# Two scans in a gated recurrence: the denominator formed in the scan's own buffer, and the key-value product moved behind the reciprocal

## The chip, the cores and the metric

One core of one Trainium2 chip runs the kernel. The time is the device time of one execution in microseconds (us), the median over runs. The engines are called PE or TensorE (matrix products; PEld is its weight loads), DVE or VectorE, ACT or ScalarE, POOL or GpSimd, and SP (it issues the DMAs).

## What is computed

The input is 8 sequences of 2048 tokens with 512 channels, in float32. A layer of gated exponential recurrence comes first, then a gated feed-forward layer, each with its residual and layer norm. The part that matters here:

```python
rkv = inputs @ W_rkv + b_rkv
r, k, v = split(rkv, 3)
r = sigmoid(r); k = exp(k); kv = k * v
# over the tokens, with one decay lam per channel
u1 = scan(lam, kv); u2 = scan(lam, k)
x = (u1 + gamma * kv) / (u2 + gamma * k + 1e-06) * r
y = layernorm(inputs + x @ W_o + b_o)
```

The feed-forward layer mixes each token of y with the one before it, takes a receptance sigmoid(xr @ W_r), keys relu(xk @ W_k) squared, and values from them through W_v.

## The kernel before

The 16384 tokens are cut into 32 blocks of 512. A block's channels stand on the 128 partitions in four chunks c = 0 to 3, the tokens in the free dimension. Each matrix product is made of float32r parts: an operand is split into a high part (a copy by ACT) and a low part (value less high part, by POOL or DVE), and a product is high x high, high x low and low x high, so a projection of one chunk is 4 x 3 = 12 matmuls of 512 columns.

**Banks.** The projections of a block are numbered n = 3c + which, with which = 0 for K, 1 for V and 2 for R, and go to PSUM bank n % 4 (`bankA`). In `project` (L1070 and on) the projection n waits until the one four places earlier has been read: K by the exponential on ACT (`key_exp`), V by the product on DVE (`kv_made`), R by the exponential of the gate on ACT (`gate_exp`).

**DVE, per chunk.** `denominator(s, c)`: the scan of the keys into `u2` (L864), the product kv = (V + bias) x key, read from PSUM (L869), a copy of u2's last column into `carry` (L872), the denominator gamma x key + u2, written over the key (L875), its product with 1 + exp(-r), which is called the gate and written in place (L879), and the reciprocal of that (L882). `numerator(s, c)`: the scan of kv into `att_f` (L890), its copy (L893) and u1 + gamma x kv (L895). The gate comes from ACT (`exp_gate`, L609 and L612), which needs the R projection of the same chunk.

**ACT and POOL.** POOL multiplies numerator and reciprocal (`att`, L413) and makes low parts (`att_low` L417, `x_low` L408, `mixed_keys_low` L440, `mixed_gate_low` L445 for xr_lo, `weight_A_low` L397, `weight_low` L403). ACT makes high parts (`att_high` L616) and the squares of the keys (`key_square`, L700 to L704).

**Order.** Each engine's order is written out by hand, in three functions per engine: `first_block`, `step` (block s beside the rest of block s - 1 and s - 2, 30 times) and `finale`. TensorE's `step` is

```python
project(s, 0, 0) ... project(s, 1, 0); attention_out(s1, 0); attention_out(s1, 1)
project(s, 1, 1); project(s, 1, 2); project(s, 2, 0); transposes(s1)
project(s, 2, 1); project(s, 2, 2); project(s, 3, 0); keys(s1)
project(s, 3, 1); receptance(s1, 0); project(s, 3, 2)
values(s1, 0); receptance(s1, 1); values(s1, 1)
```

In `first_block` the twelve projections follow each other with nothing between. In `finale` the five from (2, 1) to (3, 2) follow the transposes with nothing between; then come `keys(s1)`, the first half of `receptance(s1)` and `attention_out(s)`. Every instruction waits on its engine in that order, so a waiting one holds all behind it.

Of the kernel before, what the change touches and what calls it, by code (L numbers as in the profile page):

```python
# [24 lines left out]
ALU = mybir.AluOpType  # L25
# [4 lines left out]
NC = H // P  # L30
TB = 512
# [45 lines left out]
def wait(eng, sem, value):  # L77
    if value is not None:
        eng.wait_ge(sem, value)
# [23 lines left out]
def program(nc, xT, x, w_rkv, w_o, w_r, w_k, w_v, b_rkv, b_o, nu_log, gamma_log, mu_r, mu_k, out, seq):  # L103
# [9 lines left out]
    with ExitStack() as ctx:  # L113
# [446 lines left out]
        def _(act):  # L560
# [34 lines left out]
            def exp_key(s, c):  # L595
                act.wait_ge(k_ready, s.count(NC, c + 1))
                if s.first() and c == 0:
                    act.wait_ge(s_small, 80)

                wait(act, scale_made, s.count(NC, c - 1))  # L600
                act.activation(key[:, c % 2], bankA[(3 * c) % NBANK][:], ACT.Exp, bias=b_sb[:, 0, c:c + 1])\  # L601
                    .then_inc(key_exp, 1)

# [228 lines left out]
        def _(dve):  # L832
# [25 lines left out]
            def denominator(s, c):  # L858
                lam_c = lam[:, c:c + 1].to_broadcast([P, TB])
                dve.wait_ge(key_exp, s.count(NC, c + 1))  # L860

                wait(dve, u2_saved, s.count(NC, c))
                wait(dve, den_made, s.count(NC, c))
                dve.tensor_tensor_scan(u2[:], lam_c, key[:, c % 2], state(s, 1, c), ALU.mult, ALU.add)\  # L864
                    .then_inc(u2_scanned, 1)
                dve.wait_ge(v_ready, s.count(NC, c + 1))

                wait(dve, num_made, s.count(NC, c))
                dve.scalar_tensor_tensor(out=kv[:], in0=bankA[(3 * c + 1) % NBANK][:], scalar=b_sb[:, 1, c:c + 1],  # L869
                                         in1=key[:, c % 2], op0=ALU.add, op1=ALU.mult).then_inc(kv_made, 1)  # L870
                dve.wait_ge(u2_scanned, s.count(NC, c + 1))
                dve.tensor_copy(carry[:, 1, c:c + 1], u2[:, TB - 1:TB]).then_inc(u2_saved, 1)  # L872

                dve.wait_ge(kv_made, s.count(NC, c + 1))
                dve.scalar_tensor_tensor(out=key[:, c % 2], in0=key[:, c % 2], scalar=gamma[:, c:c + 1], in1=u2[:],  # L875
                                         op0=ALU.mult, op1=ALU.add).then_inc(den_made, 1)
                dve.wait_ge(den_made, s.count(NC, c + 1))
                dve.wait_ge(gate_plus1, s.count(NC, c + 1))
                dve.scalar_tensor_tensor(out=gate[:, c % 2], in0=key[:, c % 2], scalar=EPS_DEN, in1=gate[:, c % 2],  # L879
                                         op0=ALU.add, op1=ALU.mult).then_inc(scale_made, 1)  # L880
                dve.wait_ge(scale_made, s.count(NC, c + 1))
                dve.reciprocal(gate[:, c % 2], gate[:, c % 2]).then_inc(rec_made, 1)  # L882

            def numerator(s, c):
                lam_c = lam[:, c:c + 1].to_broadcast([P, TB])
# [83 lines left out]
            def first_block(s):  # L969
                weight_A_low(0, 0)  # L970
                x_low(s, 0)
                x_low(s, 1)
                x_low(s, 2)
                x_low(s, 3)
                weight_A_low(0, 1)
                constants()
                weight_A_low(0, 2)
                gamma_minus1()
                denominator(s, 0)
                numerator(s, 0)  # L980
                denominator(s, 1)
                numerator(s, 1)
                denominator(s, 2)
                numerator(s, 2)
                denominator(s, 3)
                numerator(s, 3)

            def step(s):
                s1, s2 = (s.back(1), s.back(2))
                if s2.exists():  # L990
                    gated_values(s2, 1)
                begin_sum(s1, 0)
                begin_sum(s1, 1)
                denominator(s, 0)
                if s2.exists():
                    statistics(s2, 1, 1, result_rows, y2_made)
                statistics(s1, 0, 0, sum_rows, ready['WO'])
                statistics(s1, 0, 1, sum_rows, ready['WO'])
                numerator(s, 0)
                denominator(s, 1)  # L1000
                mix_keys(s1)
                mix_gate(s1, 0)
                numerator(s, 1)
                denominator(s, 2)
                key_low(s1, 0)
                numerator(s, 2)
                key_low(s1, 1)
                key_low(s1, 2)
                key_low(s1, 3)
                mix_gate(s1, 1)  # L1010
                denominator(s, 3)
                gated_values(s1, 0)
                statistics(s1, 1, 0, result_rows, y2_made)
                x_low(s.back(-1), 0)
                x_low(s.back(-1), 1)
                x_low(s.back(-1), 2)
                x_low(s.back(-1), 3)
                numerator(s, 3)

            def finale(s):  # L1020
                s1, s2 = (s.back(1), s.back(2))
                begin_sum(s1, 0)
                gated_values(s2, 1)
                begin_sum(s1, 1)
                denominator(s, 0)
                statistics(s1, 0, 0, sum_rows, ready['WO'])
                statistics(s2, 1, 1, result_rows, y2_made)
                statistics(s1, 0, 1, sum_rows, ready['WO'])
                numerator(s, 0)
                denominator(s, 1)  # L1030
                numerator(s, 1)
                mix_gate(s1, 0)
                mix_keys(s1)
                denominator(s, 2)
                numerator(s, 2)
                denominator(s, 3)
                numerator(s, 3)
                begin_sum(s, 0)
                begin_sum(s, 1)
                statistics(s, 0, 0, sum_rows, ready['WO'])  # L1040
                key_low(s1, 0)
                key_low(s1, 1)
                key_low(s1, 2)
                key_low(s1, 3)
                mix_gate(s1, 1)
                statistics(s, 0, 1, sum_rows, ready['WO'])
                gated_values(s1, 0)
                mix_keys(s)
                mix_gate(s, 0)
                gated_values(s1, 1)  # L1050
                statistics(s1, 1, 0, result_rows, y2_made)
                key_low(s, 0)
                key_low(s, 1)
                mix_gate(s, 1)
                key_low(s, 2)
                key_low(s, 3)
                statistics(s1, 1, 1, result_rows, y2_made)
                gated_values(s, 0)
                gated_values(s, 1)
                statistics(s, 1, 0, result_rows, y2_made)  # L1060
                statistics(s, 1, 1, result_rows, y2_made)
                last_rows(s)
# [213 lines left out]
```

## Time and profile before

| | us |
|---|---|
| median of 3 runs | 2534.48 |
| lowest and highest | 2532.93, 2536.94 |
| the profiled execution | 2535.74 |
| its span, first to last instruction | 2533.9 |
| PE busy, DVE busy | 2510.5, 2013.6 |
| ACT busy, POOL busy | 1267.5, 1245.6 |

A matmul's row shows its start and its modelled length; matmuls are pipelined and overlap, so what counts is the distance from one start to the next. The note in brackets behind a row is the time the engine sat idle before it and what ended that.

### The profile page before, as it was taken

Reading aid. Unit: us, or ns where it says so; the run is one execution under the profiler, and the core shown is the slowest. Engines: PE = TensorE matmul, PEld = TensorE weight load, DVE = VectorE, ACT = ScalarE, POOL = GpSimd, SP = SyncE. Lnnn points to the kernel's source line nnn. Section 1 sums busy time; section 2 is a strip of 40 time slices with the busy share of each in tenths; the row PEclk is TensorE's granted clock in tenths of the full one; section 3 lists DMA queues with packets and bytes.
Section 4 is the critical chain, followed back from the end, with each engine's and each line's share of the span. In section 5 each row is a group of like instructions: output and inputs, shape, how many; then the busy total and the mean of one; then the engine's idle time right before and its main releaser. Section 6 shows DMA issues by size and latency. Waiting matters only on the chain.

```text
span 2533.9 us, 32904 instructions
## 1 busy us (share of the span) xinstructions
PE 2510.5 (99%) x11268; PEld 2076.7 (82%) x11268; DVE 2013.6 (79%) x2693; ACT 1267.5 (50%) x2157; POOL 1245.6 (49%) x1128
## 2 busy tenths in 40 slices
PE   7999999999999999999999999999999999999998
PEld 6888888888888888888888888888888888888877
DVE  7877888778787787887788777878777888787885
ACT  4545455444554444554545544455444555454545
POOL 6654454445454544535445444444444453545545
PEclk8999999999999999999999999999999999999999
DMA  4001110111100111111111011111111111110100
GB/s 170 26 34 51 45 39 34 34 51 50 34 34 34 51 51 34 46 38 35 51 39 45 34 35 50 50 34 34 35 50 50 34 43 34 43 51 34 51 25 34
DMA packets 57784, 110.63 MB, mean 44 GB/s; under 512 B 7040, under 2 KB 7040, under 8 KB 57088
## 3 DMA queue, kind: packets, MB, share of 16 engines
q1 hardware_dynamic: 57600, 108.31, 12.6%
q8 instruction: 100, 1.64, 0.3%
q14 instruction: 84, 0.69, 0.1%
HBM read 74.73 MB, written 33.55 MB: 43 GB/s over the span
## 4 chain that ended last, share of the span: by engine, by line
PE 98%; ACT 1%; POOL 0%; DVE 0%; DMA 0%; issue 0%; POOLq 0%; SPq 0%; DVEq 0%; ACTq 0%
PE bankA L1086 14%; PE bankA L1088 14%; PE bankA L1087 14%; PE bankB L1102 14%; PE bankB L1104 13%; PE bankB L1103 13%; PE bankB L1147 4%; PE bankB L1148 4%; PE bankB L1146 4%; PE bankB L1124 2%; PE bankA L1102 0%; PE bankA L1104 0%; PE bankA L1103 0%; POOL x_lo L408 0%; DMA wrkv_f<-in_w_rkv 0%; PE bankA L1148 0%
## 5 line engine op out<-in xcount | busy, mean ns | idle before, releaser
L1086 PE MATMUL bankA<-x_hi,wrkv_hi 128*128 128x512 f32 x1488 | 583.9, 392 | 4.7 <-POOL x_lo L408 4.7
L1088 PE MATMUL bankA<-x_hi,wrkv_lo 128*128 128x512 f32 x1488 | 580.5, 390 | 0.0
L1087 PE MATMUL bankA<-x_lo,wrkv_hi 128*128 128x512 f32 x1488 | 580.4, 390 | 0.0
L882 DVE RECIPROCAL gate<-gate 128x512 f32<-128x512 f32 x128 | 429.2, 3353 | 4.4
L413 POOL TENSOR_TENSOR att_f<-att_f,gate 128x512 f32<-128x512 f32 x128 | 209.4, 1636 | 280.1 <-DVE att_f L895 280.1
L1086 PEld LDWEIGHTS bankA<-x_hi,wrkv_hi 128*128 128x128 f32 x1488 | 280.3, 188 | 63.8 <-POOL x_lo L408 5.8
L1088 PEld LDWEIGHTS bankA<-x_hi,wrkv_lo 128*128 128x128 f32 x1488 | 280.1, 188 | 58.7
L1087 PEld LDWEIGHTS bankA<-x_lo,wrkv_hi 128*128 128x128 f32 x1488 | 280.4, 188 | 57.2
L424 POOL TENSOR_TENSOR ve<-mv,eps_ln 128x2 f32<-128x2 f32 x128 | 66.4, 519 | 462.6 <-DVE mv L907 459.6
L440 POOL TENSOR_TENSOR xk_lo<-xk_f,xk_hi 128x512 fp32r<-128x512 f32 x124 | 169.4, 1397 | 244.9 <-ACT xk_hi L667 244.9
L445 POOL TENSOR_TENSOR xr_lo<-xr_f,xr_hi 128x1024 fp32r<-128x1024 f32 x63 | 176.4, 2800 | 202.7 <-ACT xr_hi L672 202.7
L659 ACT ACTIVATE z<-z,shift,rstd 128x512 f32<-128x512 f32 x124 | 94.5, 809 | 297.6 <-POOL shift L433 297.6
L935 DVE SCALAR_TENSOR_TENSOR xr_f<-zT,vecs,xr_f 128x256 f32<-128x256 f32 x252 | 143.3, 628 | 123.7 <-ACT xr_f L644 123.7
L601 ACT ACTIVATE key<-bankA,b_sb 128x512 f32<-128x512 f32 x128 | 87.8, 686 | 283.9 <-PE bankA L1088 283.9
L879 DVE SCALAR_TENSOR_TENSOR gate<-key,gate 128x512 f32<-128x512 f32 x128 | 119.7, 935 | 125.4 <-ACT gate L612 123.2
L417 POOL TENSOR_TENSOR att_lo<-att_f,att_hi 128x512 fp32r<-128x512 f32 x128 | 186.8, 1460 | 32.8 <-ACT att_hi L616 32.8
L1102 PE MATMUL bankB<-wr_hi,xr_hi 128*128 128x512 f32 x504 | 199.5, 396 | 1.1 <-POOL xr_lo L445 1.1
L1103 PE MATMUL bankB<-wr_lo,xr_hi 128*128 128x512 f32 x504 | 196.4, 390 | 0.0
L1104 PE MATMUL bankB<-wr_hi,xr_lo 128*128 128x512 f32 x504 | 196.3, 389 | 0.0
L1102 PE MATMUL bankB<-wo_hi,att_hi 128*128 128x512 f32 x496 | 192.9, 389 | 0.0
L1103 PE MATMUL bankB<-wo_lo,att_hi 128*128 128x512 f32 x496 | 192.9, 389 | 0.0
L1104 PE MATMUL bankB<-wo_hi,att_lo 128*128 128x512 f32 x496 | 192.9, 389 | 0.0
(150 smaller groups left out, 5588.5 us busy)
## 6 DMA issues: line engine op xcount, KB each, us to landing
y<-in_x SPq DMA_DIRECT2D x128, 256.0 KB, 2.7
x_f<-in_xT SPq DMA_DIRECT2D x124, 256.0 KB, 4.0
out<-z SPq DMA_DIRECT2D x124, 256.0 KB, 2.1
wrkv_f<-in_w_rkv SPq DMA_DIRECT2D x3, 768.0 KB, 7.7
xk_f<-in_xT SPq DMA_DIRECT2D x4, 256.0 KB, 4.5
wo_f<-in_w_o SPq DMA_DIRECT2D x1, 1024.0 KB, 11.2
wk_f<-in_w_k SPq DMA_DIRECT2D x1, 1024.0 KB, 13.1
wr_f<-in_w_r SPq DMA_DIRECT2D x1, 1024.0 KB, 15.2
```

The lines of the kernel that those rows point to most:

```text
L413: pool.tensor_tensor(att_f[:, c], att_f[:, c], gate[:, c % 2], ALU.mult).then_inc(att_made, 1)
L417: pool.tensor_tensor(att_lo[:, c], att_f[:, c], att_hi[:, c], ALU.subtract).then_inc(att_lo_made, 1)
L440: pool.tensor_tensor(lo[:, c], value[:, c], hi[:, c], ALU.subtract).then_inc(xk_lo_made, 1)
L445: pool.tensor_tensor(lo[:], value[:], hi[:], ALU.subtract).then_inc(xr_lo_made, 1)
L882: dve.reciprocal(gate[:, c % 2], gate[:, c % 2]).then_inc(rec_made, 1)
L935: dve.scalar_tensor_tensor(out=value[:, c], in0=zT[:, c, HALF * half + 1:HALF * half + HALF + 1], scalar=vecs[:, 2, c:c + 1], in1=value[:, ...
L1086: pe.matmul(bank[:], w_hi, hi[:, h], start=(h == 0), stop=False)
L1087: pe.matmul(bank[:], w_hi, lo[:, h], start=False, stop=False)
L1088: last = pe.matmul(bank[:], w_lo, hi[:, h], start=False, stop=(h == NC - 1))
L1102: pe.matmul(bank[:], hi, w_hi[:, c], start=(c == 0 and not begun), stop=False, skip_group_check=begun)
L1103: pe.matmul(bank[:], hi, w_lo[:, c], start=False, stop=False, skip_group_check=begun)
L1104: last = pe.matmul(bank[:], lo, w_hi[:, c], start=False, stop=(c == NC - 1), skip_group_check=begun)
```

## The change

The four DVE instructions of the denominator now follow the key scan directly, and the denominator is written into `u2`, the scan's own buffer, so that the key stays whole. The product kv moves into a function of its own, `product`, which every order calls straight behind `denominator`; it stands there behind the reciprocal. The scan of a chunk waits for the gate's product of the chunk before (`scale_made`), which is now u2's last reader. On ACT the exponential of a key, which writes the key's buffer, waits for `den_made` and `kv_made` of two chunks earlier in place of `scale_made`.

```diff
@@ exp_key
-                wait(act, scale_made, s.count(NC, c - 1))
+                wait(act, den_made, s.count(NC, c - 1))
+                wait(act, kv_made, s.count(NC, c - 1))
@@ denominator
-                wait(dve, u2_saved, s.count(NC, c))
-                wait(dve, den_made, s.count(NC, c))
+                wait(dve, scale_made, s.count(NC, c))
                 dve.tensor_tensor_scan(u2[:], lam_c, key[:, c % 2], state(s, 1, c), ALU.mult, ALU.add)\
                     .then_inc(u2_scanned, 1)
+                dve.wait_ge(u2_scanned, s.count(NC, c + 1))
+                dve.tensor_copy(carry[:, 1, c:c + 1], u2[:, TB - 1:TB]).then_inc(u2_saved, 1)
+                dve.wait_ge(u2_saved, s.count(NC, c + 1))
+                dve.scalar_tensor_tensor(out=u2[:], in0=key[:, c % 2], scalar=gamma[:, c:c + 1], in1=u2[:],
+                                         op0=ALU.mult, op1=ALU.add).then_inc(den_made, 1)
+                dve.wait_ge(den_made, s.count(NC, c + 1))
+                dve.wait_ge(gate_plus1, s.count(NC, c + 1))
+                dve.scalar_tensor_tensor(out=gate[:, c % 2], in0=u2[:], scalar=EPS_DEN, in1=gate[:, c % 2],
+                                         op0=ALU.add, op1=ALU.mult).then_inc(scale_made, 1)
+                dve.wait_ge(scale_made, s.count(NC, c + 1))
+                dve.reciprocal(gate[:, c % 2], gate[:, c % 2]).then_inc(rec_made, 1)
+
+            def product(s, c):
                 dve.wait_ge(v_ready, s.count(NC, c + 1))
+                dve.wait_ge(key_exp, s.count(NC, c + 1))
 
                 wait(dve, num_made, s.count(NC, c))
                 dve.scalar_tensor_tensor(out=kv[:], in0=bankA[(3 * c + 1) % NBANK][:], scalar=b_sb[:, 1, c:c + 1],
                                          in1=key[:, c % 2], op0=ALU.add, op1=ALU.mult).then_inc(kv_made, 1)
-                dve.wait_ge(u2_scanned, s.count(NC, c + 1))
-                dve.tensor_copy(carry[:, 1, c:c + 1], u2[:, TB - 1:TB]).then_inc(u2_saved, 1)
-
-                dve.wait_ge(kv_made, s.count(NC, c + 1))
-                dve.scalar_tensor_tensor(out=key[:, c % 2], in0=key[:, c % 2], scalar=gamma[:, c:c + 1], in1=u2[:],
-                                         op0=ALU.mult, op1=ALU.add).then_inc(den_made, 1)
...
@@ the orders, at each of the twelve calls of denominator
                 denominator(s, 0)
+                product(s, 0)
```

How DVE's order moves, first in the first block, chunk 0 and the start of chunk 1. Before:

```order
L864 SCALAR_TENSOR_TENSOR u<-lam,key 128x512
L869 SCALAR_TENSOR_TENSOR kv<-bankA,b_sb,key 128x512
L872 COPY carry<-u 128x1
L875 SCALAR_TENSOR_TENSOR key<-key,gamma,u 128x512
L879 SCALAR_TENSOR_TENSOR gate<-key,gate 128x512
L882 RECIPROCAL gate<-gate 128x512
L890 SCALAR_TENSOR_TENSOR att_f<-lam,kv 128x512
L893 COPY carry<-att_f 128x1
L895 SCALAR_TENSOR_TENSOR att_f<-kv,gamma,att_f 128x512
L864 SCALAR_TENSOR_TENSOR u<-lam,key 128x512
L869 SCALAR_TENSOR_TENSOR kv<-bankA,b_sb,key 128x512
```

And with the change (lines are those of the changed kernel):

```order
L864 SCALAR_TENSOR_TENSOR u<-lam,key 128x512
L867 COPY carry<-u 128x1
L869 SCALAR_TENSOR_TENSOR u<-key,gamma,u 128x512
L873 SCALAR_TENSOR_TENSOR gate<-u,gate 128x512
L876 RECIPROCAL gate<-gate 128x512
L883 SCALAR_TENSOR_TENSOR kv<-bankA,b_sb,key 128x512
L892 SCALAR_TENSOR_TENSOR att_f<-lam,kv 128x512
L895 COPY carry<-att_f 128x1
L897 SCALAR_TENSOR_TENSOR att_f<-kv,gamma,att_f 128x512
L864 SCALAR_TENSOR_TENSOR u<-lam,key 128x512
L867 COPY carry<-u 128x1
```

The row of kv went from behind the first scan to behind the reciprocal, ahead of the numerator's scan.

In the last block, on DVE, from the reciprocal of chunk 1 to that of chunk 2 (xr_f and xk_f are the gate and key mixing of the block before). Before:

```order
L882 RECIPROCAL gate<-gate 128x512
L890 SCALAR_TENSOR_TENSOR att_f<-lam,carry,kv 128x512
L893 COPY carry<-att_f 128x1
L895 SCALAR_TENSOR_TENSOR att_f<-kv,gamma,att_f 128x512
L935 SCALAR_TENSOR_TENSOR xr_f<-zT,vecs,xr_f 128x256 x4
L927 SCALAR_TENSOR_TENSOR xk_f<-zT,vecs,xk_f 128x512 x4
L864 SCALAR_TENSOR_TENSOR u<-lam,carry,key 128x512
L869 SCALAR_TENSOR_TENSOR kv<-bankA,b_sb,key 128x512
L872 COPY carry<-u 128x1
L875 SCALAR_TENSOR_TENSOR key<-key,gamma,u 128x512
L879 SCALAR_TENSOR_TENSOR gate<-key,gate 128x512
L882 RECIPROCAL gate<-gate 128x512
```

And with the change:

```order
L876 RECIPROCAL gate<-gate 128x512
L883 SCALAR_TENSOR_TENSOR kv<-bankA,b_sb,key 128x512
L892 SCALAR_TENSOR_TENSOR att_f<-lam,carry,kv 128x512
L895 COPY carry<-att_f 128x1
L897 SCALAR_TENSOR_TENSOR att_f<-kv,gamma,att_f 128x512
L937 SCALAR_TENSOR_TENSOR xr_f<-zT,vecs,xr_f 128x256 x4
L929 SCALAR_TENSOR_TENSOR xk_f<-zT,vecs,xk_f 128x512 x4
L864 SCALAR_TENSOR_TENSOR u<-lam,carry,key 128x512
L867 COPY carry<-u 128x1
L869 SCALAR_TENSOR_TENSOR u<-key,gamma,u 128x512
L873 SCALAR_TENSOR_TENSOR gate<-u,gate 128x512
L876 RECIPROCAL gate<-gate 128x512
```

The kv of chunk 1 came into this stretch, ahead of the numerator of chunk 1, and the kv of chunk 2 moved out of it, behind its last row. On TensorE nothing moves.

## Rows read from the trace of the kernel before

**Rows 1.** The page: engine totals, and the chain that ended last, by engine.

```profile
PE 2510.5 (99%) x11268; PEld 2076.7 (82%) x11268; DVE 2013.6 (79%) x2693; ACT 1267.5 (50%) x2157; POOL 1245.6 (49%) x1128
...
PE 98%; ACT 1%; POOL 0%; DVE 0%; DMA 0%; issue 0%; POOLq 0%; SPq 0%; DVEq 0%; ACTq 0%
```

**Rows 2.** TensorE's waits: released by, us in total, times, longest.

```profile
PE bankA L1086 <- POOL x_lo L408: 4.7, 2, 4.1
```

**Rows 3.** TensorE's timeline, first block: start, length, instruction, [idle before <-releaser].

```profile
23.37 0.39 PE L1086 MATMUL bankA<-xk_hi,wrkv_hi 128*128 128x512 f32 x1
...
23.60 0.39 PE L1087 MATMUL bankA<-xk_lo,wrkv_hi 128*128 128x512 f32 x1
...
31.53 0.39 PE L1086 MATMUL bankA<-xk_hi,wrkv_hi 128*128 128x512 f32 x1
...
43.89 0.77 PE L1086 MATMUL bankA<-xk_hi,wrkv_hi 128*128 128x512 f32 x1 [4.04 <-POOL wrkv_lo L397]
```

**Rows 4.** DVE, first block: both reciprocals; kv's line over the run, ns min/median/max.

```profile
L869 DVE SCALAR_TENSOR_TENSOR kv<-bankA,b_sb,key x128: 718/726/731, 16.0 to 2452.8; 128x512 f32<-128x512 f32 x128
...
20.67 3.35 DVE L882 RECIPROCAL gate<-gate 128x512 f32<-128x512 f32 x1
...
30.34 3.35 DVE L882 RECIPROCAL gate<-gate 128x512 f32<-128x512 f32 x1
```

**Rows 5.** ACT's timeline, first block: the exponential of chunk 3's key.

```profile
37.17 0.69 ACT L601 ACTIVATE key<-bankA,b_sb 128x512 f32<-128x512 f32 x1 [1.36 <-PE bankA L1088]
```

**Rows 6.** Two stretches: PE, PEld, DVE, ACT, POOL busy (instructions), granted clock, DMA, GB/s.

```profile
43.90:49.30 5.40, 5.40 (x13) 4.24 (x14) 5.25 (x7) 0.00 (x0) 4.14 (x2) 0.50 0.00 0
...
2457.60:2466.00 8.40, 6.50 (x28) 5.03 (x28) 7.34 (x8) 7.22 (x14) 4.07 (x3) 1.00 0.23 62
```

**Rows 7.** A middle block: DVE's reciprocal of chunk 1, TensorE's R of chunk 2.

```profile
2352.88 3.35 DVE L882 RECIPROCAL gate<-gate 128x512 f32<-128x512 f32 x1
...
2357.45 0.39 PE L1086 MATMUL bankA<-x_hi,wrkv_hi 128*128 128x512 f32 x1
```

**Rows 8.** Middle block: DVE, POOL, TensorE at the receptance; then last block, DVE and POOL.

```profile
2384.33 1.28 DVE L864 TENSOR_TENSOR_SCAN u<-lam,carry,key 128x512 f32<-128x512 f32 x1
...
2387.08 0.69 DVE L879 SCALAR_TENSOR_TENSOR gate<-key,gate 128x512 f32<-128x512 f32 x1
...
2387.23 2.80 POOL L445 TENSOR_TENSOR xr_lo<-xr_f,xr_hi 128x1024 fp32r<-128x1024 f32 x1 [6.68 <-ACT xr_hi L672]
...
2390.09 0.49 PE L1102 MATMUL bankB<-wr_hi,xr_hi 128*128 128x512 f32 x1
...
2390.42 0.39 PE L1103 MATMUL bankB<-wr_lo,xr_hi 128*128 128x512 f32 x1
...
2455.27 3.35 DVE L882 RECIPROCAL gate<-gate 128x512 f32<-128x512 f32 x1
...
2456.34 2.37 POOL L445 TENSOR_TENSOR xr_lo<-xr_f,xr_hi 128x1024 fp32r<-128x1024 f32 x1
```

**Rows 9.** Last block: DVE, TensorE and ACT.

```profile
2441.34 1.27 DVE L864 TENSOR_TENSOR_SCAN u<-lam,carry,key 128x512 f32<-128x512 f32 x1
...
2445.99 3.35 DVE L882 RECIPROCAL gate<-gate 128x512 f32<-128x512 f32 x1
...
2458.54 1.26 DVE L890 TENSOR_TENSOR_SCAN att_f<-lam,carry,kv 128x512 f32<-128x512 f32 x1
...
2443.98 0.39 PE L1086 MATMUL bankA<-x_hi,wrkv_hi 128*128 128x512 f32 x1
...
2458.86 0.47 PE L1102 MATMUL bankB<-wr_hi,xr_hi 128*128 128x512 f32 x1 [1.12 <-POOL xr_lo L445]
...
2465.34 0.47 PE L1102 MATMUL bankA<-wo_hi,att_hi 128*128 128x512 f32 x1 [0.78 <-POOL att_lo L417]
...
2457.78 0.60 ACT L700 ACTIVATE xk_f<-bankB 128x512 f32<-128x512 f32 x1 [3.15 <-PE bankB L1148]
...
2463.23 0.62 ACT L616 ACTIVATE att_hi<-att_f 128x512 fp32r<-128x512 f32 x1
```

More of the change, by code:

```diff
@@ L870, in denominator @@
                                          in1=key[:, c % 2], op0=ALU.add, op1=ALU.mult).then_inc(kv_made, 1)
-                dve.wait_ge(u2_scanned, s.count(NC, c + 1))
-                dve.tensor_copy(carry[:, 1, c:c + 1], u2[:, TB - 1:TB]).then_inc(u2_saved, 1)
-                dve.wait_ge(kv_made, s.count(NC, c + 1))
-                dve.scalar_tensor_tensor(out=key[:, c % 2], in0=key[:, c % 2], scalar=gamma[:, c:c + 1], in1=u2[:],
-                                         op0=ALU.mult, op1=ALU.add).then_inc(den_made, 1)
[L877 to L882, printed above, removed]
             def numerator(s, c):
@@ L979, in first_block @@
                 denominator(s, 0)
+                product(s, 0)
                 numerator(s, 0)
                 denominator(s, 1)
+                product(s, 1)
                 numerator(s, 1)
                 denominator(s, 2)
+                product(s, 2)
                 numerator(s, 2)
                 denominator(s, 3)
+                product(s, 3)
                 numerator(s, 3)
@@ L994, in step @@
                 denominator(s, 0)
+                product(s, 0)
                 if s2.exists():
@@ L1000, in step @@
                 denominator(s, 1)
+                product(s, 1)
                 mix_keys(s1)
@@ L1004, in step @@
                 denominator(s, 2)
+                product(s, 2)
                 key_low(s1, 0)
@@ L1011, in step @@
                 denominator(s, 3)
+                product(s, 3)
                 gated_values(s1, 0)
@@ L1025, in finale @@
                 denominator(s, 0)
+                product(s, 0)
                 statistics(s1, 0, 0, sum_rows, ready['WO'])
@@ L1030, in finale @@
                 denominator(s, 1)
+                product(s, 1)
                 numerator(s, 1)
@@ L1034, in finale @@
                 denominator(s, 2)
+                product(s, 2)
                 numerator(s, 2)
                 denominator(s, 3)
+                product(s, 3)
                 numerator(s, 3)
```

## The prediction

> **What bounds the kernel now.** I read the engine totals first, then the chain that ended last, and then what TensorE waited for. TensorE is busy 99% of the span and 98% of the chain is its own [rows 1]. Its longest waits stand in the first block: 4.7 us in two for x_lo [rows 2] and 4.04 us for a low part of the projection weights [rows 3]; in the last block one of 1.12 and one of 0.78 us follow [rows 9]. Elsewhere its matmuls start every 0.227 us (23.37 to 23.60 [rows 3]), and DVE, ACT and POOL run beside them. So the change, which adds and removes no instruction, can only cost time where TensorE comes to wait longer, and only give time where it waits now. 0.2% of the time, 5.1 us, is about what a measurement here tells from no change.
>
> **What moves.** The product kv (L869 before) stood second in each chunk, behind the scan; now it stands behind the reciprocal. kv_made is not only read by the numerator: it also frees the bank of V for the projection four places later. K, V and R of chunks 0 to 3 are twelve projections of 12 matmuls (2.72 us each at 0.227), so kv of chunk 0 gates R of chunk 1, kv of chunk 1 gates R of chunk 2, kv of chunk 2 gates R of chunk 3, and kv of chunk 3 gates R of chunk 0 in the next block. The reciprocal lasts 3.35 us and lets the next instruction start 3.27 us after its own start (2455.27 to 2458.54) [rows 8, 9]; kv lasts 0.73 us in each of its 128 runs [rows 4]; and TensorE's matmul starts 0.15 us behind the end of what it waited for (xr_lo in the last block, 2456.34 + 2.37 = 2458.71 [rows 8], against 2458.86 [rows 9]). So **the bank is free 3.27 + 0.73 + 0.15 = 4.15 us after the reciprocal starts**. Worse, the reciprocal needs the gate, which needs R of its own chunk. I go through the gated projections.
>
> **First block.** The reciprocal of chunk 0 starts at 20.67 [rows 4] and nothing in front of it moves, because it is the gate that comes late; kv used to run in time that was otherwise spent waiting. The bank is now free at 24.82; R of chunk 1 started at 23.37 [rows 3]. First stall: 1.45 us. R of chunk 1 then ends 1.45 us later, and with it the exponential of its gate. The second reciprocal, which started at 30.34 [rows 4] behind VectorE's own chain and not behind the gate, does not take that on in full; I put it between 30.0 and 30.6. Bank free 34.15 to 34.75, against the start of R of chunk 2 at 31.53 [rows 3] plus the 1.45: second stall 1.2 to 1.8 us. Together 2.6 to 3.2, I take **2.9 us**. Is it hidden by the 4.04 us wait at 43.89 [rows 3]? That wait ends with POOL's wrkv_lo, which is queued behind wo_lo, which needs wo_hi from ACT, which is queued behind the exponential of chunk 3's key, and that one waited 1.36 us for TensorE (37.17) [rows 5]. The chain starts at TensorE, so it is handed on. R of chunk 3 still waits for POOL (to 46.8 by this), not for its kv.
>
> **Middle, what it costs.** Tightest is R of chunk 2: reciprocal of chunk 1 at 2352.88, bank free at 2357.03, matmul due at 2357.45 [rows 7]: 0.42 us in hand. I read the same two times in all 30 blocks; what is in hand lies between 0.42 and 0.57. The others have microseconds. The key mixing behind it starts some 0.3 us later, under ACT's two passes over the same chunks. Cost taken as zero; cover 0.42 us.
>
> **Middle, what it gives.** Near the end of each block the second half of the receptance needs xr_lo. POOL takes 2.80 us for it when it begins 0.15 us into VectorE's gate product (2387.23 against 2387.08), and 2.37 us when it runs wholly under a reciprocal (2456.34 under 2455.27) [rows 8]. Here TensorE reaches that matmul a little before xr_lo: the matmul at 2390.09 is followed by the next after 0.33 us in place of 0.227 [rows 8], and so in each of the 30 blocks, with 0.10 to 0.13 us lost. Now the gate product starts earlier. Scan, copy and denominator take about 2.3 us from 2384.33 in place of 2.75 with kv between them, so the product runs from about 2386.6 to 2387.3 and is over as xr_lo begins; xr_lo ends 0.3 to 0.4 us sooner and the loss goes: 30 x 0.11 = **3.3 us back** (bounds 0 and 3.9). The Trainium skill (SBUF — State Buffer, on the shared GPSIMD/Vector port) says that a VectorE instruction with two SBUF inputs and a GpSimd instruction that reads SBUF exclude each other for a whole instruction, while one with a single SBUF input does not. The 2.80 and the 2.37 agree with it. By the page the same lock also speaks against the change: kv reads one operand from PSUM and so left POOL a gap, and the denominator that now follows the scan can find the port taken. By that rule the stall below would be its upper bound of 7.5 us and the sum 2544.1.
>
> **Last block.** This is the dear place. VectorE runs without a gap here, so kv of chunk 1, now ahead of the numerator, shifts the scan of chunk 2 from 2441.34 to 2442.04. Scan start to reciprocal start was 4.65 us (2441.34 to 2445.99) [rows 9]; kv goes out (0.7), the copy and the denominator now each wait for the one in front (back 0.2, what the scan's 1.28 us [rows 8] and the copy's handovers allow). Reciprocal at 2446.2, bank free at 2450.4. R of chunk 3 started at 2443.98 [rows 9], just behind the old kv: **stall 6.4 us** (5.5 if the contended gate product of 1.7 us gets off free, 7.5 if POOL slips in once more). Behind it stand keys, receptance and the output projection. The latter needs att_lo of chunk 3, which follows att_hi (2463.23), which is queued on ACT behind three key squares that began at 2457.78 when the keys had ended [rows 9]. So it comes 7.6 us behind the end of the keys, now as before, and the waits of 1.1 and 0.8 us that stand there take nothing off.
>
> **The clock.** After the 4.04 us wait in the first block the granted clock was 0.50, i.e. 1.2 GHz, from 43.9 to 49.3; 13 matmuls fill those 5.40 us [rows 6], against 2.95 at 0.227: 2.5 us lost. Behind the waits of 1.12 and 0.78 us in the last block it stayed at 1.00, i.e. 2.4 GHz [rows 6]. A wait of 6.4 us is beyond the one that cost it, so I add **2.5 us** for the last block (bounds 0 and two such falls, 5.0, since a second wait of about 2.2 us opens before the output projection). The first block's new waits of 1.45 and 1.5 us are nearer to 1.12 than to 4.04: zero.
>
> **Sum.** 2.9 + 6.4 + 2.5 - 3.3 = +8.5 us. The profiled execution took 2535.74 (span 2533.9 and 1.8 around it), 1.3 above the median of 2534.48; the sum gives 2544.2 for such an execution and **2543.0** for the median.
>
> **Rivals.**
> *The waits already there swallow the late product (not slower).* If the POOL chain in the first block and the att_lo chain in the last did not start at TensorE, the first block would cost nothing (4.04 us cover 2.9) and the last 6.4 - 1.9 = 4.5, with the clock kept. Sum 4.5 - 3.3 = +1.2, 2535.7. Against it: both chains lead back to TensorE in the rows. It decides where the delay handed on falls below 2 us in the last block.
> *More of the clock.* Each of the three short new waits (two in the first block, one before the output projection) that also costs the clock adds 2.5: 2545.5 to 2550.5. For it: nothing shows what 1.5 to 2.2 us do.
> *xr_lo stays late.* If its 2.80 us are due to the reciprocal or ACT is what is late, nothing comes back: 2546.3. Against it: the 2.37 us under a reciprocal.
> *R of chunk 2 late in every block.* If the gate's chain slips past the 0.42 us in hand by the port or by a longer handover, each 0.3 us late costs 30 x 0.3 = 9 us: 2552.
>
> **Chances.** Forecast 0.50; swallowed 0.12; more of the clock 0.16; xr_lo stays 0.12; chunk 2 late 0.08; 0.02 for more given back than 5 us. The range 2538.5 to 2551 takes in the first four but the low end of the swallowed case: its low end is the forecast with the stall at 5.5 and no fall of the clock (2539.6) and a little. Slower by over 0.2% means above 2539.6: 0.86; within 0.2%: 0.12; faster: 0.02.
>
> **What would show it.** Right: among TensorE's waits a new one of about 6.4 us for kv near 2450 and two near 24.8 and 34.5 of 1.4 and 1.5 us; clock 0.50 right behind the long one; xr_lo near 2.4 us and no 0.33 us step at the receptance; each middle block shorter by 0.11 us. Wrong: a wait for kv in the middle blocks, or no wait for kv at all.

## The result, and the profile after

| | before | after |
|---|---|---|
| median of 17 runs, us | 2533.82 | 2541.00 |
| lowest, us | 2532.93 | 2539.19 |
| profiled execution, us | 2535.74 | 2541.62 |
| its span, us | 2533.9 | 2539.8 |

The medians differ by 7.2 us. The ratio, which is not formed from the two medians, is 1.0023 with a 95% interval of 1.0017 to 1.0030: slower by 5.8 us, between 4.3 and 7.6. The prediction said 2543.0, +8.5 us, and gave 0.86 to slower. One of the 17 executions of the changed kernel took 3528.65 us at a mean clock of 0.67 and is left out of the ratio, as is one of the kernel before in the last comparison below (5095.76 us at 0.46).

The two profiled executions differ by 5.9 us, so the difference can be read off between them. The first question is what TensorE waits for. The list of its waits (released by, us in total, times, longest), where before there were only x_lo and wrkv_lo, one xr_lo and one att_lo [rows 2, 3, 9]:

```profile
PE bankA L1100 <- DVE kv L883: 8.9, 3, 6.6
PE bankB L1108 <- ACT wrkv_hi L575: 6.3, 1, 6.3
PE bankA L1100 <- POOL wrkv_lo L397: 4.7, 1, 4.7
PE bankA L1100 <- POOL x_lo L408: 4.5, 2, 4.2
PE bankA L1116 <- POOL att_lo L417: 1.2, 1, 1.2
PE bankB L1116 <- ACT xk_f L701: 0.7, 1, 0.7
```

Three waits for kv, 8.9 us in all, and none in the 30 middle blocks. Where they stand, in TensorE's timeline of the changed kernel (start, length, instruction, idle time before it and its releaser):

```profile
24.79 0.50 PE L1100 MATMUL bankA<-xk_hi,wrkv_hi 128*128 128x512 f32 x1 [1.14 <-DVE kv L883]
...
34.48 0.50 PE L1100 MATMUL bankA<-xk_hi,wrkv_hi 128*128 128x512 f32 x1 [1.20 <-DVE kv L883]
...
47.61 0.77 PE L1100 MATMUL bankA<-xk_hi,wrkv_hi 128*128 128x512 f32 x1 [4.67 <-POOL wrkv_lo L397]
...
2440.46 0.39 PE L1102 MATMUL bankA<-x_hi,wrkv_lo 128*128 128x512 f32 x1
2447.46 0.80 PE L1100 MATMUL bankA<-x_hi,wrkv_hi 128*128 128x512 f32 x1 [6.61 <-DVE kv L883]
2448.05 0.63 PE L1101 MATMUL bankA<-x_lo,wrkv_hi 128*128 128x512 f32 x1
2448.48 0.63 PE L1102 MATMUL bankA<-x_hi,wrkv_lo 128*128 128x512 f32 x1
```

The first two answer to R of chunks 1 and 2 at 23.37 and 31.53 [rows 3], the third to 43.89 [rows 3], the long one to 2443.98 [rows 9]. Behind the long one matmuls start 0.43 us apart, at the lower of the clock's two levels, as the granted clock of 0.50 in this stretch says (columns as in [rows 6]):

```profile
2447.46:2452.30 4.84, 4.84 (x11) 3.84 (x12) 4.67 (x6) 0.00 (x0) 2.19 (x1) 0.50 0.01 3
```

I cut both executions at two marks, the transposes of the first and of the last step, and take TensorE's first matmul as the start:

| stretch | before, us | after, us | difference |
|---|---|---|---|
| start to first transposes (first block and a piece) | 6.04 to 87.89 = 81.85 | 6.26 to 89.32 = 83.06 | +1.2 |
| 30 middle blocks | 87.89 to 2431.26 = 2343.37 | 89.32 to 2427.95 = 2338.63 | -4.7 |
| last block, to the end of the span | 102.64 | 111.85 | +9.2 |

With the 0.2 us by which the start itself differs this is the 5.9 us. A middle block takes 77.95 us on the mean in place of 78.11. Most of the reason stands where the prediction looked for it. VectorE, POOL and TensorE of the changed kernel at the receptance of a middle block, answering to the same block of before [rows 8]:

```profile
2383.46 0.69 DVE L873 SCALAR_TENSOR_TENSOR gate<-u,gate 128x512 f32<-128x512 f32 x1
2384.19 3.35 DVE L876 RECIPROCAL gate<-gate 128x512 f32<-128x512 f32 x1
```

```profile
2384.07 2.41 POOL L445 TENSOR_TENSOR xr_lo<-xr_f,xr_hi 128x1024 fp32r<-128x1024 f32 x1 [6.43 <-ACT xr_hi L673]
```

```profile
2386.93 0.39 PE L1116 MATMUL bankB<-wr_hi,xr_hi 128*128 128x512 f32 x1
2387.16 0.39 PE L1117 MATMUL bankB<-wr_lo,xr_hi 128*128 128x512 f32 x1
```

The gate product is nearly over (2384.15) when POOL begins, xr_lo takes 2.41 us in place of 2.80 and is there 0.45 us before TensorE wants it, and the matmuls start 0.23 us apart with no step. In all 30 middle blocks together, the four steps from the matmul ahead of this one to the third behind it are 3.8 us longer than 4 x 0.227 before, and 0.0 us longer now: 3.8 of the 4.7 us.

### The profile page after: what moved, and what is told of

Its sections match the earlier page's. It is cut to its first block and busy times, and to the rows that moved or that the text cites. A ratio compares the mean times of both kernels' runs of the same rounds, so it can differ in the third digit from the quotient of the medians.

```text
span 2539.8 us, 32912 instructions
## 1 busy us (share of the span) xinstructions
PE 2506.9 (99%) x11268; PEld 2079.3 (82%) x11268; DVE 2046.9 (81%) x2693; ACT 1266.2 (50%) x2157; POOL 1240.7 (49%) x1128
## 5 line engine op out<-in xcount | busy, mean ns | idle before, releaser
L440 POOL TENSOR_TENSOR xk_lo<-xk_f,xk_hi 128x512 fp32r<-128x512 f32 x124 | 178.7, 1471 | 245.0 <-ACT xk_hi L668 245.0
L445 POOL TENSOR_TENSOR xr_lo<-xr_f,xr_hi 128x1024 fp32r<-128x1024 f32 x63 | 164.8, 2616 | 197.4 <-ACT xr_hi L673 197.4
L937 DVE SCALAR_TENSOR_TENSOR xr_f<-zT,vecs,xr_f 128x256 f32<-128x256 f32 x252 | 153.1, 667 | 114.0 <-ACT xr_f L645 114.0
L873 DVE SCALAR_TENSOR_TENSOR gate<-u,gate 128x512 f32<-128x512 f32 x128 | 120.0, 937 | 137.5 <-ACT gate L613 135.3
L1161 PE MATMUL bankB<-xk_lo,wk_hi 128*128 128x512 f32 x496 | 193.0, 389 | 0.0
L1162 PE MATMUL bankB<-xk_hi,wk_lo 128*128 128x512 f32 x496 | 193.0, 389 | 0.0
L1118 PE MATMUL bankB<-wv_hi,xk_lo 128*128 128x512 f32 x496 | 193.0, 389 | 0.0
```

What stands on the lines that cost most here:

```text
L440: pool.tensor_tensor(lo[:, c], value[:, c], hi[:, c], ALU.subtract).then_inc(xk_lo_made, 1)
L1118: last = pe.matmul(bank[:], lo, w_hi[:, c], start=False, stop=(c == NC - 1), skip_group_check=begun)
L1161: pe.matmul(bank[:], wk_hi[:, c, cols], lo[:, c], start=False, stop=False)
L1162: last = pe.matmul(bank[:], wk_lo[:, c, cols], hi[:, c], start=False, stop=(c == NC - 1))
```

## Experiments

All kernels below are made from the changed one by a switch that says for each block and chunk where kv stands: behind the reciprocal (late, as in the change) or right behind the key scan (early, as before). The denominator is formed in u2 in all of them.

```diff
+            def late(s, c):
+                return c in (FIRST if s.first() else LAST if s.last() else MIDDLE)
+
             def denominator(s, c):
...
                     .then_inc(u2_scanned, 1)
+                if not late(s, c):
+                    product_now(s, c)
                 dve.wait_ge(u2_scanned, s.count(NC, c + 1))
...
-            def product(s, c):
+            def product_now(s, c):
...
+            def product(s, c):
+                if late(s, c):
+                    product_now(s, c)
```

Each comparison gives the median, and the ratio to the kernel before on the same chip with its 95% interval. The middle in the table is the stretch between the two marks of the result's table, in the profiled execution.

| kernel | median | before | ratio | middle |
|---|---|---|---|---|
| early everywhere | 2536.26 | 2534.91 | 1.0006 [0.9997, 1.0015] | 2345.33 |
| late in the middle | 2530.42 | 2534.91 | 0.9981 [0.9972, 0.9990] | 2338.79 |
| late in the last block | 2545.36 | 2534.91 | 1.0039 [1.0025, 1.0052] | 2345.15 |
| late in the first block | 2537.66 | 2534.91 | 1.0012 [1.0003, 1.0021] | 2345.10 |
| middle, chunk 3 alone | 2530.32 | 2534.49 | 0.9983 [0.9974, 0.9992] | 2339.91 |
| middle, chunks 0 to 2 | 2535.32 | 2534.49 | 1.0003 [0.9994, 1.0012] | 2344.97 |
| late in the middle, kv of chunk 1 twice | 2539.55 | 2534.49 | 1.0016 [1.0007, 1.0025] | 2347.37 |
| the change, last wait filled | 2539.71 | 2534.49 | 1.0019 [1.0010, 1.0028] | 2338.45 |
| last block, chunk 2 alone | 2543.83 | 2534.79 | 1.0035 [1.0023, 1.0046] | 2345.63 |
| last block, chunk 1 alone | 2536.64 | 2534.79 | 1.0009 [0.9999, 1.0019] | 2345.14 |
| middle chunk 3, first waits filled | 2526.16 | 2534.79 | 0.9963 [0.9948, 0.9977] | 2338.83 |
| the same, first block late | 2529.26 | 2534.79 | 0.9977 [0.9967, 0.9986] | 2338.45 |

The middle falls into two groups: 2338.45 to 2339.91 us in the kernels with kv of chunk 3 late there (the one with kv of chunk 1 twice aside), and 2344.97 to 2345.63 us in the six with it early. The kernel before has 2343.37.

**The buffer without the move.** FIRST = MIDDLE = LAST = ().

```diff
+                return c in (() if s.first() else () if s.last() else ())
```

> The change without its move: the denominator is formed in u2, but kv stands right behind the key scan in every block, as before. Theory (all of the difference comes from where kv stands): same as before within 1 us, no wait of TensorE for kv, xr_lo at 2.8 us in the middle. Rival (the buffer counts: two handovers more in the chain, another buffer under the port): 1 to 4 us off the kernel before, on either side.

The interval of the ratio holds 1, and the median is 1.3 us up, a little more than was expected. TensorE waits for no kv. The middle is 2.0 us longer than before, 0.07 us a block. These rows show the cause. VectorE, POOL and TensorE of this kernel, the middle block of [rows 8]:

```profile
2387.27 0.69 DVE L878 SCALAR_TENSOR_TENSOR gate<-u,gate 128x512 f32<-128x512 f32 x1
```

```profile
2387.36 2.87 POOL L445 TENSOR_TENSOR xr_lo<-xr_f,xr_hi 128x1024 fp32r<-128x1024 f32 x1 [6.68 <-ACT xr_hi L673]
```

```profile
2390.28 0.50 PE L1125 MATMUL bankB<-wr_hi,xr_hi 128*128 128x512 f32 x1
2390.62 0.39 PE L1126 MATMUL bankB<-wr_lo,xr_hi 128*128 128x512 f32 x1
```

The copy and the denominator now each wait for the one in front, so the gate product stands a few hundredths later against xr_lo: xr_lo begins 0.09 or 0.10 us into it in 23 of the 30 blocks (0.15 or 0.16 in the other seven), where before it was 0.14 to 0.16 in 23 and 0.21 or 0.22 in seven. It then takes 2.87 us in place of 2.80; over all its runs its median is 2851 ns against 2812 before. The four steps at the receptance lose 5.6 us in the 30 blocks against 3.8, which is nearly all of the 2.0. So the buffer by itself gives nothing and costs the middle 2.0 us; it only makes the move possible, and the move by itself is worth 6.5 us in the middle (2345.33 to 2338.79), of which 4.6 show against the kernel before.

**The middle alone.** MIDDLE = (0, 1, 2, 3).

```diff
+                return c in (() if s.first() else () if s.last() else (0, 1, 2, 3))
```

> kv behind the reciprocal in the 30 middle blocks only, right behind the scan in the first and the last block. Theory: the middle alone gives time, 30 x 0.11 to 0.16 us, so 3.3 to 4.8 us faster than before, 2529 to 2530.5, and no wait of TensorE for kv. Rival (the shorter middle of the changed kernel is the shadow of its shifted first block): no gain, 2533 to 2534.

Faster than before, 0.9981. The middle takes 2338.79 us, as in the changed kernel (2338.63). The shorter middle is not a shadow of the first block: it comes with the late kv in the middle itself.

**The last block alone.** LAST = (0, 1, 2, 3).

```diff
+                return c in (() if s.first() else (0, 1, 2, 3) if s.last() else ())
```

> kv behind the reciprocal in the last block only. Theory: one wait of 6.6 us for kv, clock 0.50 behind it, 9.2 us slower than before, 2543. Rival (waits that stood there swallow part): 4 to 7 us slower.

9.1 us above the kernel with kv early everywhere, 10.4 above the kernel before, which is 1.2 more than was expected and about what the buffer adds. The waits and two stretches of this kernel (PE, PEld, DVE, ACT and POOL busy, granted clock, DMA):

```profile
PE bankA L1109 <- DVE kv L888: 6.6, 1, 6.6
```

```profile
2450.00:2457.00 7.00, 4.21 (x12) 3.37 (x13) 6.77 (x8) 0.00 (x0) 4.18 (x3) 0.57 0.01 2
2457.00:2463.00 6.00, 6.00 (x28) 4.97 (x27) 5.09 (x4) 1.84 (x3) 4.07 (x3) 1.00 0.00 0
```

The one wait of 6.6 us and the low clock behind it are there without any change in the other blocks. The waits that stood later swallowed nothing: the stretch from the last transposes to the end of the span is 111.03 us against 102.65 with kv early everywhere, 8.4 us, and R of chunk 3 started 6.77 us late and seven slow matmuls lost 1.6, which is 8.3.

**The first block alone.** FIRST = (0, 1, 2, 3).

```diff
+                return c in ((0, 1, 2, 3) if s.first() else () if s.last() else ())
```

> kv behind the reciprocal in the first block only. Theory: two waits of 1.1 and 1.2 us for kv, 2.9 us in all with the restarts, handed on to POOL's chain; the clock's low stretches shift and may give some back, so 1.4 to 3 us slower than before, 2535 to 2537. Rival (the 4 us wait for wrkv_lo swallows them): within 0.5 us.

2.4 us of waits for kv, and 1.4 us more than with kv early everywhere, 2.7 more than before. That the difference between 2.9 and 1.4 is the clock was only a guess at this point; the last two experiments are about that.

**Chunk 3 of the middle, and chunks 0 to 2.** MIDDLE = (3,), then MIDDLE = (0, 1, 2).

```diff
+                return c in (() if s.first() else () if s.last() else (3,))
```

> As the kernel with kv late in the middle blocks only, but for chunk 3 alone; chunks 0 to 2 keep kv right behind the key scan. Theory (the gain is the gate product of chunk 3 getting out of the way of POOL's xr_lo): the whole gain stays, 2529 to 2531, xr_lo at 2.4 us. Rival (the gain is a freer gate chain in all chunks): a quarter of it, 2533 to 2534.

```diff
+                return c in (() if s.first() else () if s.last() else (0, 1, 2))
```

> The counterpart: kv late in chunks 0 to 2 of the middle blocks, early in chunk 3. Theory: no gain, the time of the kernel with kv early everywhere, 2534 to 2536.5, xr_lo at 2.8 us. Rival: three quarters of the gain, 2531 to 2532.

Chunk 3 alone has the time of all four, 0.9983 against 0.9981; chunks 0 to 2 alone have none of the gain. xr_lo, all its runs (ns min/median/max), first with chunk 3 late, then with chunks 0 to 2 late:

```profile
L445 POOL TENSOR_TENSOR xr_lo<-xr_f,xr_hi x63: 2369/2412/2854, 104.1 to 2492.1; 128x1024 fp32r<-128x1024 f32 x63
```

```profile
L445 POOL TENSOR_TENSOR xr_lo<-xr_f,xr_hi x63: 2369/2847/2876, 106.6 to 2499.3; 128x1024 fp32r<-128x1024 f32 x63
```

Median 2412 with the gain and 2847 without: time and xr_lo go together, and only the chunk whose gate product meets xr_lo moves either.

**The cover of R of chunk 2.** As late in the middle, with one kv more in chunk 1.

```diff
+                if c == 1 and not s.first() and not s.last():
+                    dve.wait_ge(v_ready, s.count(NC, c + 1))
+                    dve.wait_ge(key_exp, s.count(NC, c + 1))
+                    wait(dve, num_made, s.count(NC, c))
+                    dve.scalar_tensor_tensor(out=kv[:], in0=bankA[(3 * c + 1) % NBANK][:],
+                                             scalar=b_sb[:, 1, c:c + 1], in1=key[:, c % 2],
+                                             op0=ALU.add, op1=ALU.mult).then_inc(pad_made, 1)
+                    dve.wait_ge(pad_made, s.count(1, 0))
```

> kv late in the middle blocks only, and there in chunk 1 the kv product is made twice, so that kv_made comes about 0.7 us later still. Theory (R of chunk 2 is covered by 0.4 to 0.6 us and by no more): TensorE waits for kv in all 30 blocks, 0.1 to 0.3 us each, 3 to 9 us above the kernel with kv late in the middle, 2533.5 to 2539.5. Rival (the cover is wider than the rows say, for the banks free earlier or the wait is absorbed later): no change, 2530.5.

9.1 us slower than without it; the middle grew by 8.6 us, 0.29 a block. The waits of the weight loads in this kernel:

```profile
PEld bankA L1118 <- DVE kv L897: 12.3, 30, 0.5
```

Thirty waits, one per middle block. Kv of chunk 1 and the start of R of chunk 2, first in the kernel with kv late in the middle, then in this one:

```profile
2351.64 0.65 DVE L888 SCALAR_TENSOR_TENSOR kv<-bankA,b_sb,key 128x512 f32<-128x512 f32 x1
...
2352.94 0.39 PE L1109 MATMUL bankA<-x_hi,wrkv_hi 128*128 128x512 f32 x1
```

```profile
2360.19 0.65 DVE L889 SCALAR_TENSOR_TENSOR kv<-bankA,b_sb,key 128x512 f32<-128x512 f32 x1
2360.87 0.75 DVE L897 SCALAR_TENSOR_TENSOR kv<-bankA,b_sb,key 128x512 f32<-128x512 f32 x1
...
2361.26 0.39 PE L1120 MATMUL bankA<-x_hi,wrkv_lo 128*128 128x512 f32 x1
2361.68 0.50 PE L1118 MATMUL bankA<-x_hi,wrkv_hi 128*128 128x512 f32 x1
2362.02 0.39 PE L1119 MATMUL bankA<-x_lo,wrkv_hi 128*128 128x512 f32 x1
```

Without the second kv, R started 0.65 us behind the end of kv (0.64 to 0.81 over the 30 blocks). With it, R started 0.06 us behind (0.05 or 0.06 in all 30). So about 0.6 us had been in hand. The second kv ends 0.78 us behind the first; that is about 0.2 us too late for TensorE, and the step behind the wait (0.34 in place of 0.227) brings it to the 0.29 us a block. This rival was 0.6 us away from being the result.

**The last wait filled.** The changed kernel, with 30 matmuls in the last block ahead of R of chunk 3, into a bank that the keys overwrite.

```diff
+            def fill(n):
+                pe.wait_ge(zT_copied, Step(per_batch, s=blocks - 2, blocks=blocks).count(NT, NT))
+                for _ in range(n):
+                    pe.matmul(bankB[3][:], wk_hi[:, 0, 0:P], x_hi[:, 0], start=True, stop=True)
...
                 project(s, 3, 1)
+                fill(30)
                 project(s, 3, 2)
```

> The changed kernel with 30 more matmuls in the last block, into a bank that the keys overwrite next, ahead of the projection that waits for kv, so that TensorE works through its wait (30 x 0.227 = 6.8 us). Theory (2.3 us of the last block's loss are the clock): granted clock 1.00 throughout the last block, 10 slow matmuls fewer, 2.0 to 2.5 us faster than the changed kernel, 2538 to 2539, in spite of 30 matmuls more. Rival (the matmuls behind the wait are slow for another reason, or the fall is not due to the idle time): same as the changed kernel or slower, 2541 and up.

The last block took 109.66 us from the transposes (2426.14) to the end of the span (2535.8), 2.2 us less than in the changed kernel, with 30 matmuls more. Its clock in that stretch:

```profile
2440.00:2460.00 20.00, 19.61 (x86) 15.69 (x84) 19.48 (x17) 2.33 (x5) 13.24 (x8) 1.00 0.02 5
```

1.00 throughout. So in this pair of profiles 2.2 of the 9.2 us are the clock, and the rest the wait. The size is not fixed, though: the same wait was followed by 11 matmuls at the lower level in the changed kernel (2.4 us lost) and by seven in the kernel with the last block late alone (1.6 us lost, a last block of 111.03 us, 1.4 more than here). The median, 2539.71, lies 0.7 us above what was expected and is 1.3 us below that of the changed kernel, which was timed in another comparison; against the kernel before in each, the ratios are 1.0019 and 1.0023, with intervals that overlap. The share of the clock rests on the profiled stretch, not on the medians.

**Chunks 2 and 1 of the last block.** LAST = (2,), then LAST = (1,).

```diff
+                return c in (() if s.first() else (2,) if s.last() else ())
```

> kv behind the reciprocal in the last block's chunk 2 alone. Theory: this one product makes the long wait; without chunk 1's kv ahead of it the scan of chunk 2 starts 0.6 us earlier, so the wait for kv is 5.9 to 6.1 us in place of 6.6, and the time 8 to 9 us above kv early everywhere (2536), 2543.5 to 2545. Rival (chunks 1 and 2 share the loss): a wait of 3 to 5 us.

```diff
+                return c in (() if s.first() else (1,) if s.last() else ())
```

> kv behind the reciprocal in the last block's chunk 1 alone. Theory: R of chunk 2 has 1 us in hand there, and the 0.6 us by which chunk 2's kv comes later just eats what R of chunk 3 has: a wait of 0 to 0.4 us, time within 1 us of kv early everywhere, 2535.5 to 2537. Rival: 3 to 4 us slower.

Chunk 2 alone waits 5.8 us and has nearly the whole loss, 1.0035 of 1.0039. Chunk 1 alone shows no wait of TensorE for kv in the list (R of chunk 3 starts with steps of 0.38 and 0.34 us at 2444.9, where 0.227 is usual) and has 1.0009, as near to kv early everywhere (1.0006) as can be told.

**The first block with the clock out of play.** Two kernels with matmuls in its two waits of 4 us, into a bank that the next block's sum overwrites. MIDDLE = (3,), LAST = (); FIRST = () and then (0, 1, 2, 3), there with 20 in the first wait.

```diff
+            def fill(n):
+                for _ in range(n):
+                    pe.matmul(bankB[3][:], wrkv_hi[:, 0, 0, 0], wrkv_hi[:, 0, 0], start=True, stop=True)\
+                        .then_inc(columns_written, 1)
...
-                        dve.wait_ge(columns_written, NBANK)
+                        dve.wait_ge(columns_written, NBANK + 36)
...
                 for h in range(NC):
+                    if n == 0 and s.batch is None and s.s == 1 and h == 2:
+                        fill(18)
...
                 project(s, 3, 1)
+                fill(18)
                 project(s, 3, 2)
```

> The kernel with kv late in chunk 3 of the middle blocks alone, and with 18 idle matmuls in each of the first block's two 4 us waits of TensorE (for wrkv_lo and for x_lo), into a bank that the next block overwrites. Theory (those waits cost the clock, and the slow matmuls behind them lie on the chain TensorE, ACT, POOL): clock 1.00 from 12 us on, 4 to 6 us faster than without the filling (2530.3), 2524.5 to 2526.5, the fastest of all. Rival (POOL's chain alone sets the first block's end): no gain.

> The same with kv late in the first block too, and 20 idle matmuls in the first wait. Theory (the first block's late kv costs 2.9 us, of which the changed kernel shows less because its waits shift the clock's low stretches): with the clock out of play the whole 2.5 to 3 us show against the kernel before this one, 2527 to 2529. Rival (the first block absorbs part of it): 0 to 1.5 us.

The stretch from 12 to 60 us of five kernels, same columns as above: before, the changed one, late in the first block, and the two filled ones (kv early, kv late).

```profile
12.00:60.00 48.00, 39.29 (x151) 31.01 (x150) 41.92 (x40) 21.82 (x27) 35.03 (x22) 0.85 0.38 149
```

```profile
12.00:60.00 48.00, 36.53 (x146) 28.45 (x145) 40.43 (x36) 21.70 (x27) 31.08 (x21) 0.93 0.38 150
```

```profile
12.00:60.00 48.00, 36.59 (x145) 28.39 (x144) 42.23 (x38) 21.46 (x27) 32.95 (x21) 0.94 0.38 149
```

```profile
12.00:60.00 48.00, 47.51 (x207) 38.37 (x206) 42.57 (x41) 23.38 (x29) 36.68 (x23) 1.00 0.41 159
```

```profile
12.00:60.00 48.00, 45.00 (x194) 35.68 (x193) 43.96 (x40) 21.48 (x27) 33.81 (x22) 1.00 0.39 152
```

With the waits filled the clock stays at 1.00, and the late first block costs 3.1 us between the medians (2529.26 less 2526.16) and 2.6 us between the marks (start to first transposes 79.14 against 76.55). Without filling, the granted clock is 0.85 before and 0.93 and 0.94 with kv late in the first block: its shifted waits happened to leave fewer matmuls at the low level. From 20 us on, those matmuls lost 5.9 us in the kernel before, 4.1 in the changed one, 2.8 with the first block late alone. The low stretches are not a fixed property of a kernel, though: the same sum is 5.9 us in three more and 4.0 to 5.3 in five of the unfilled kernels that leave the first block's order as it was. With it subtracted, start to first transposes is 75.4 to 76.2 us in all nine of these with kv early there, and 77.9 to 79.0 in the three unfilled ones with kv late.

The first of the two filled kernels is the fastest of all, 0.9963 of before, 2526.16 us.

## Why the prediction was right, point by point

The forecast of +8.5 us lies a little above the measured 5.8 (4.3 to 7.6). Stretch by stretch, in the profiled executions: +1.2 in the first block where 2.9 was forecast, -4.7 in the middle where -3.3 was, +9.2 in the last block where 8.9 was.

**TensorE bounds it, so only its waits count: right.** VectorE's busy time rose from 2013.6 to 2046.9 us, and that shows only where TensorE comes to wait: in 8.9 us of waits for kv.

**First block, two stalls, 2.9 us: right in size, and partly given back.** Between matmul starts the two stalls are 1.53 and 1.59 us, 2.66 more than the usual distances, and the next matmul each time comes 0.1 us late as well: 2.9. They were handed on through the chain that was named: the exponential of chunk 3's key ran at 40.25, having waited 1.36 us for TensorE as before [rows 5]. R of chunk 3 then started at 47.61, 3.5 us later than before when both are counted from the first matmul, for POOL's wrkv_lo took 2.19 us there in place of 1.25. What the step left out is that the low-clock stretches would move too; they gave 1.8 of it back in the profiled execution (5.9 to 4.1 us). The prediction put a clock term only on the side of a loss. This is the term of the sum that was off: +2.9 measured as +1.2. That single pair of profiles is partly luck: start to first transposes is 79.5 to 82.0 us in the nine unfilled kernels with kv early in the first block and 81.1 to 83.1 in the three with kv late. With the clock out of play the 2.9 stands, as 2.6 between the marks and 3.1 between the medians.

**Middle, nothing lost: right**, with about 0.6 us to spare where 0.42 was worked out. The 4.15 us from the reciprocal's start to the free bank were too many: kv's row is 0.65 us there and not 0.73, and TensorE starts 0.05 us behind it where 0.15 had been read off xr_lo, so it is 3.98 us (2443.48 to 2447.46 in the last block).

**Middle, 3.3 us back: right in mechanism, low in size.** The middle gave 4.7. 0.11 us a block was read off one matmul's delay; behind it several more matmuls each came 0.01 us late, and four blocks of the kernel before took 78.2 to 78.4 us where nearly all of the changed one's take 77.92 to 77.96. Experiments tie the gain to chunk 3 and to xr_lo. In three of the four longer blocks of before the extra time stands where the next block's first projection begins (steps of 0.36 and 0.33 us at 2088.7 in the longest); what held it there is not known. The rule of the Trainium skill (SBUF — State Buffer, Who interferes with whom) holds in these rows: an instruction of VectorE with two SBUF inputs, begun first, delays xr_lo, and a reciprocal, with one input, does not (2.41). The delay is what is left of the gate product less 0.14 us or so: xr_lo takes 2.75 us when it begins 0.21 us into it, 2.80 at 0.15 and 2.87 at 0.09. Its other side shows in the last block, where the denominator of chunk 2 took 1.41 us against 0.75 for one that met no POOL instruction.

**Last block, 6.4 us stall and 2.5 us clock: right.** 6.77 us, and 2.2 to 2.4 us in the changed kernel (1.6 behind the same wait in another). VectorE of the changed kernel, the last block's chunk 2, against the scan at 2441.34 and the reciprocal at 2445.99 [rows 9] (the changed kernel is 3.3 us ahead at this place):

```profile
2438.88 1.27 DVE L864 TENSOR_TENSOR_SCAN u<-lam,carry,key 128x512 f32<-128x512 f32 x1
2440.18 0.15 DVE L867 COPY carry<-u 128x1 f32<-128x1 f32 x1
2440.37 1.41 DVE L869 SCALAR_TENSOR_TENSOR u<-key,gamma,u 128x512 f32<-128x512 f32 x1
2441.81 1.63 DVE L873 SCALAR_TENSOR_TENSOR gate<-u,gate 128x512 f32<-128x512 f32 x1
2443.48 3.35 DVE L876 RECIPROCAL gate<-gate 128x512 f32<-128x512 f32 x1
2446.75 0.65 DVE L883 SCALAR_TENSOR_TENSOR kv<-bankA,b_sb,key 128x512 f32<-128x512 f32 x1
```

The rows between that scan and that reciprocal in the kernel before:

```profile
2442.53 0.72 DVE L869 SCALAR_TENSOR_TENSOR kv<-bankA,b_sb,key 128x512 f32<-128x512 f32 x1
2443.18 0.14 DVE L872 COPY carry<-u 128x1 f32<-128x1 f32 x1
2443.29 0.97 DVE L875 SCALAR_TENSOR_TENSOR key<-key,gamma,u 128x512 f32<-128x512 f32 x1
2444.29 1.67 DVE L879 SCALAR_TENSOR_TENSOR gate<-key,gate 128x512 f32<-128x512 f32 x1
```

Scan to reciprocal is 4.60 us where 4.2 was worked out. Taking kv out brought the copy 0.54 us nearer to the scan (1.84 to 1.30); the handover from the copy took 0.08 of it back, and the denominator, met by POOL's xk_lo, 0.44 (1.44 us from its start to the gate product's, in place of 1.00). With the scan another 0.15 us later than worked out, the reciprocal came 0.6 us later, the bank was free 0.2 us sooner behind it, and 6.4 became 6.8. The stall was handed on in full, through the key squares on ACT, as these rows of the changed kernel say, against 2457.78 and 2463.23 [rows 9] (5.9 us later, and with the 3.3 us that it was ahead 9.2):

```profile
2463.70 0.60 ACT L701 ACTIVATE xk_f<-bankB 128x512 f32<-128x512 f32 x1 [9.05 <-PE bankB L1162]
...
2469.16 0.62 ACT L617 ACTIVATE att_hi<-att_f 128x512 fp32r<-128x512 f32 x1
```

The waits there changed their names (0.7 for the keys' bank, 1.2 for att_lo, in place of 1.1 for xr_lo and 0.8), and their sum stayed at 1.9 us. No second fall of the clock came, since no wait of 2.2 us opened.

**The rivals.** "Swallowed" fell with the last block alone: the stall and the slow matmuls came to 8.3 us, and the last block was 8.4 us longer. "xr_lo stays late" fell with chunk 3. "R of chunk 2 late in every block" did not happen but was made to happen by 0.8 us. "More of the clock" fell: the new waits of 1.14 and 1.20 us left the granted clock at 1.00 from 20 to 43 us, and it was 1.00 around the waits before the output projection too.

## What to carry to other kernels

Ask of a moved instruction not only who uses its result but who waits for what it frees: here the product's reader lost nothing, and the bank's next writer lost 6.8 us at the place in the last block where five projections stand in a row. An order tuned for the steady step must be asked again at the first and the last block, where the cover is other work; here the same move was worth -4.7 us in the middle and +9.2 in the last block, and keeping it only for chunk 3 of the middle turned a loss of 0.2% into a gain of 0.2%. Where one engine's instruction takes longer beside another's, the few tenths can be had by moving the neighbour, with no work removed.

## What the runs showed that was not expected

Work that is thrown away can save time. Thirty matmuls into a bank that is overwritten took 2.2 us off the last block of the changed kernel (1.4 against the kernel with the last block late alone), and 36 in the first block's two waits took the kernel from 2530.3 to 2526.2 us (two comparisons, 0.9983 and 0.9963 of before). In the two profiles of that pair the stretch to the first transposes is 3.0 us shorter with the waits filled (79.53 to 76.55), where the slow matmuls had lost 4.0; another 1.1 us of their difference stands in the middle, where nothing was filled. No wait of up to 1.3 us that stood alone was followed by the lower level in any of these kernels; every one of about 4 us and more that was not filled was, in some kernels right behind it and in others up to 2.8 us later, for 6 to 15 matmuls.

A matmul behind a wait starts its successor 0.30 to 0.34 us later in place of 0.227, even at the full clock, so each short wait costs 0.1 us beyond itself. And kv's row is 0.73 us long behind a scan and 0.65 behind a reciprocal with the same operands. That is no gain for what follows it on VectorE, which starts 0.65 us after kv's start in the one case (2442.53 to 2443.18) and 0.74 in the other (2446.75 to 2447.49).
